# Long cross attention: rounds of two key tiles, with score halves issued beside peak halves and one visit to the full array in a round

## What is computed

```python
q = _rope((x_query @ Wq.T)...); k = _rope((x_kv @ Wk.T)...); v = (x_kv @ Wv.T)...
attn = softmax(einsum('bhqd,bhkd->bhqk', q, k) * SCALE)      # 56 queries x 1500 keys x 16 heads
out = einsum('bhqk,bhkd->bhqd', attn, v) ... @ Wo.T
```

## Time and profile before

| what | value |
|---|---|
| median of the three runs | 1459.55 us (1456.22 to 1461.99) |
| span of the profiled execution, first to last instruction | 1397.8 us |
| the profiled execution's own time end to end | not given; the median is 61.75 us above the span |
| TensorE matmuls busy, whole span | 1277.9 us, 91% |
| VectorE, ScalarE, GpSimd busy | 76%, 57%, 60% |
| first and last score load of the stage | 605.4 us, 1293.6 us |

### The profile page before, as it was taken

The page is one execution under the profiler, slowest core; times in us unless marked ns, Lnnn a source line. Parts: engine busy times, 40 slices in busy tenths (PEclk is TensorE's granted clock), DMA queues, the critical chain, the costliest instruction groups (busy, mean ns, idle before and its releaser), DMA issues.

```text
span 1397.8 us, 42378 instructions
## 1 busy us (share of the span) xinstructions
PE 1277.9 (91%) x17390; PEld 904.3 (65%) x17390; DVE 1066.3 (76%) x1817; ACT 802.5 (57%) x1760; POOL 842.5 (60%) x839
## 2 busy tenths in 40 slices
PE   6878999998997898678999999999999999988998
PEld 4556888788984666345565666656656666565986
DVE  6895676766677888777888888888888887886556
ACT  2542335336662333147677777777777777777541
POOL 6676232161567566578677786776777767665033
PEclk9887999999998999879999999999999999999999
DMA  5002700004521504546765465565565654546112
GB/s 139 2 1 68 244 3 2 2 28 131 163 59 29 78 12 89 104 133 134 156 136 145 118 129 134 113 139 130 112 145 133 114 139 96 120 85 186 43 49 54
DMA packets 84849, 136.19 MB, mean 97 GB/s; under 512 B 19809, under 2 KB 68322, under 8 KB 81314
## 3 DMA queue, kind: packets, MB, share of 16 engines
q1 hardware_dynamic: 80946, 125.87, 38.7%
q0 software_dynamic: 3712, 7.61, 1.9%
HBM read 98.38 MB, written 40.76 MB: 100 GB/s over the span
## 4 chain that ended last, share of the span: by engine, by line
PE 44%; ACT 6%; DVE 3%; issue 2%; POOL 2%; DMA 1%; ACTq 0%; POOLq 0%; SPq 0%; DVEq 0%
PE ps L2024 9%; PE ps L2040 8%; PE ps L1986 6%; PE ps L1977 6%; PE ps L2000 4%; ACT ARENA L2196 3%; ACT ARENA L2180 2%; PE ps L2502 2%; PE ps L2466 2%; DVE ARENA L2117 2%; PE ps L2513 1%; PE ps L2049 1%; PE ps L2476 1%; POOL ARENA L2245 1%; DMA key_parts<-ARENA 1%
## 5 line engine op out<-in xcount | busy, mean ns | idle before, releaser
L2117 DVE TENSOR_REDUCE ARENA<-ps 112x2 f32<-112x1000 f32 x384 | 456.3, 1197 | 109.7 <-PE ps L2000 108.0
L2196 ACT ACTIVATE ARENA<-ps 125x448 f32<-125x448 f32 x768 | 375.8, 546 | 106.5 <-PE ps L2024 103.7
L2245 POOL TENSOR_TENSOR ARENA<-ARENA 64x500 f32<-64x500 f32 x192 | 219.9, 1145 | 33.5 <-ACT ARENA L2174 9.1
L2024 PEld LDWEIGHTS ps<-ARENA 64*125 64x125 bf16 x3072 | 123.2, 134 | 143.3 <-ACT ARENA L2196 98.4
L2040 PE MATMUL ps<-ARENA 125*17 125x112 f32 x6144 | 210.3, 263 | 0.0
L2024 PE MATMUL ps<-ARENA 64*125 64x112 bf16 x3072 | 167.5, 228 | 28.7 <-ACT ARENA L2196 24.8
L2040 PEld LDWEIGHTS ps<-ARENA 125*17 125x17 f32 x6144 | 129.4, 97 | 57.3 <-issue 48.0
L2000 PE MATMUL ps<-ARENA 64*112 64x500 bf16 x768 | 153.7, 385 | 9.8 <-DVE ARENA L2117 8.9
L130 POOL TENSOR_TENSOR rs<-rs,mhalf 128x1 f32<-128x1 f32 x96 | 73.0, 762 | 122.4 <-DVE rs L125 122.1
L2251 POOL TENSOR_TENSOR ARENA<-ARENA 128x500 f32<-128x500 f32 x96 | 136.8, 1425 | 7.5
L2256 POOL TENSOR_TENSOR ARENA<-ARENA 128x500 bf16<-128x500 f32 x96 | 104.1, 1085 | 57.4 <-ACT ARENA L2180 57.4
(11 more groups left out here) (332 smaller groups left out, 2401.7 us busy)
## 6 DMA issues: line engine op xcount, KB each, us to landing
ARENA<-key_parts SPq DMA_DIRECT2D x192, 187.5 KB, 4.9
ARENA<-in_ctxT SPq DMA_DIRECT2D x96, 250.0 KB, 3.2
key_parts<-ARENA SPq DMA_DIRECT2D x64, 375.0 KB, 3.9
slots<-in_c_blank SPq DMA_DIRECT2D x2, 1472.0 KB, 12.8
results<-ARENA SPq DMA_DIRECT2D x42, 64.0 KB, 2.7
last_slots<-in_c_blank SPq DMA_DIRECT2D x1, 2144.0 KB, 12.5
ARENA<-in_L_ffn_W SPq DMA_DIRECT2D x1, 2048.0 KB, 8.5
ARENA<-in_L_ffn_W SPq DMA_DIRECT2D x4, 512.0 KB, 10.6
```

The source lines that it names most:

```text
L2024: m = e.matmul(ps[0:KT, b1[h], 112 * g:112 * g + 112], KS[b % 4][r, g, KT * kt:KT * kt + KT], Q1[r, b % 2, 112 * g:112 * g + 112], start=T ...
L2117: e.tensor_reduce(mxp[0:112, b % 2, 2 * g:2 * g + 2, ch], ps[0:112, b1:b1 + 2, 0:500], AX, ALU.max) \
L2196: e.activation(Pb[0:KT, n % NP_, 448 * h:448 * h + 448], ps[0:KT, b1[h], 0:448], ACT.Exp, bias=0.0, scale=1.0).then_inc(exped.sem, 1)
L2245: e.tensor_tensor(T2[r:r + 64, :], T0[64 - r:128 - r, n % 2, :], sin[64 - r:128 - r, sl], ALU.mult) \
```

## The change

The list `order()` now goes in rounds of two tiles m and m+1: score m, peak, score m+1, peak, then in one visit all steps of the kinds in VISIT (of both tiles: keys, values, full, fold, turn, out, finish and others), then apply m-2 and apply m-1. Steps of tile m that are not in VISIT stay between the two scores; those of tile m+1 come behind the visit. Banks are dealt out from the new list by the same rule.

On TensorE a score that is followed by a peak is now issued with it, by a new function. For each half h of the score: its first matmul, then one peak matmul of 500 columns in the other half of the rows, then the score's other three. The wait for a bank is made for each half by itself.

```diff
--- before.py
+++ after.py
@@ -1776,6 +1776,8 @@
                     f[10].append(("turn_slots", 1))
                 return f
 
+            VISIT = ("keys", "values", "full", "fold", "turn", "out", "finish", "query", "route", "count", "turn_slots")
+
             def order():
                 yield from (("clear", 0), ("mask", 0), ("mask", 1), ("keys", 2, 0), ("keys", 2, 1))
                 for k in range(12):
@@ -1793,26 +1795,26 @@
                     yield ("stack", 2, i)
                 for k in range(6):
                     yield ("peak", 1, k)
-                for n in range(B * NK + 2):
-                    b, kt = divmod(n, NK)
-                    if n < B * NK:
+                for m in range(0, B * NK + 2, 2):
+                    visit = []
+                    for n in (m, m + 1) if m < B * NK else ():
+                        b, kt = divmod(n, NK)
                         yield ("score", b, kt)
                         if kt < 6 and b + 1 < B:
                             yield ("peak", b + 1, 6 + kt)
                         if kt >= 6 and b + 2 < B:
                             yield ("peak", b + 2, kt - 6)
-                    steps = side(b)[kt] if n < B * NK else []
-                    short = [x for x in steps if kt % 2 and x[0] in ("full", "fold", "turn", "out", "finish", "query")]
-                    if n >= 3 and n % 2:
-                        yield ("apply", *divmod(n - 3, NK))
-                        yield from short
-                        yield ("apply", *divmod(n - 2, NK))
-                        if kt == 1:
-                            yield ("own", b - 1)
-                    singles = [x for x in steps if x[0] in ("keys", "values")]
-                    yield from singles
-                    yield from [x for x in steps if x not in short and x not in singles]
-                    if n == B * NK:
+                        steps = side(b)[kt]
+                        visit += [x for x in steps if x[0] in VISIT]
+                        if n % 2:
+                            yield from visit
+                        yield from [x for x in steps if x[0] not in VISIT]
+                    if m >= 2:
+                        yield ("apply", *divmod(m - 2, NK))
+                        yield ("apply", *divmod(m - 1, NK))
+                        if m % NK == 0:
+                            yield ("own", m // NK - 1)
+                    if m == B * NK:
                         yield ("begin", 0)
 
             def early(t):
@@ -2065,10 +2067,45 @@
                 elif kind in ("route", "count", "turn_slots", "begin"):
                     stages[5].parts["step_pe"](e, w, step, b1)
 
+            def score_beside_peak(e, w, step, beside):
+                b, kt = step[1:]
+                pb, p = beside[1:]
+                pg, ch = divmod(p, 3)
+                n, sb, pk = NK * b + kt, at[step], at[beside]
+                w.wait_ge(*ks_of(b))
+                w.wait_ge(*q_full(b + 1))
+                w.wait_ge(*ks_of(pb))
+                if pb == 3:
+                    w.wait_ge(*c2_in(2))
+                w.wait_ge(*masked(pb + 1))
+                for h in range(2):
+                    own, other = slice(64 * h, 64 * h + 64), slice(64 - 64 * h, 128 - 64 * h)
+                    if free[sb[h]]:
+                        w.wait_ge(*free[sb[h]])
+                    free[sb[h]] = exped(2 * n + h + 1)
+                    w.wait_ge(*free[pk + 1 - h])
+                    for g in range(4):
+                        m = e.matmul(ps[0:KT, sb[h], 112 * g:112 * g + 112], KS[b % 4][own, g, KT * kt:KT * kt + KT],
+                                     Q1[own, b % 2, 112 * g:112 * g + 112], start=True, stop=True)
+                        if g == 3:
+                            m.then_inc(scored.sem, 1)
+                        if g == 0:
+                            m = e.matmul(ps[0:112, pk + 1 - h, 0:500], Q0[other, pb % 3, pg].rearrange("p j s -> p (j s)"),
+                                         KS[pb % 4][other, pg, 500 * ch:500 * ch + 500], start=True, stop=True)
+                            if h:
+                                m.then_inc(peak_mm.sem, 1)
+                free[pk] = free[pk + 1] = peaked(12 * pb + p + 1)
+
             def pe(e, w):
                 w.wait_ge(*c1_in(len(loads)))
-                for step in order():
-                    pe_step(e, w, step)
+                steps = list(order())
+                taken = None
+                for step, after in zip(steps, steps[1:] + [("end", 0)]):
+                    if step[0] == "score" and after[0] == "peak":
+                        score_beside_peak(e, w, step, after)
+                        taken = after
+                    elif step != taken:
+                        pe_step(e, w, step)
 
             def early_pe(e, w, t):
                 for step in early(t):
```

## The result

The changed kernel takes 1475.65 us (median of four runs, 1470.9 to 1476.07) against 1457.88 us for the kernel before, timed beside it: a ratio of 1.0124, 95% interval 1.0094 to 1.0154. It is 18 us slower, where 22 us were forecast.

A forecast was written before the change was run, and what follows sets the result against it. TensorE's order of work was taken to set the pace. 24 batches at +0.98 (+23.6), +2 for batches 0 to 2 and 26, -2.7 and -1 at the end gave +22 on 1459.55: 1481.5 us, range 1464 to 1525.

The forecast's parts named there:

- The ring (Part 3): Three banks: second half of score m+1 and the visit wait for tile m's exponentials; visit starts at 1.62, not 1.02.
- Changes of shape (Part 2): TensorE's rounds have three changes of block shape for four: -0.13 us; fold, full, out, finish another -0.26; turn only -0.13.
- Halves (Part 1): Score halves issued beside peak halves on TensorE: each half still has 0.43 us to do, no gain booked.
- Other queues: GpSimd, VectorE, ScalarE's cast and SyncE: zero cost, covered by the longer round; otherwise a late cast holds the odd tile's exponentials.
- The sum: Whole kernel: 24 batches times 0.98 is +23.6, with the remaining batches and rounds together +22 us.
- The stage's remaining parts: Batches 0 to 2 and 26 take +2 together, nine rounds from batch 28 -2.7, the last nine rounds -1.
- Two readings of the old trace: TensorE's clock at nine tenths or more all through the stage; median of runs 61.75 us above the profiled span.
- The 61.75 us between the span and the median: Median of the runs over the profiled span of the kernel before; left alone, with the profile's end-to-end time not shown.
- A: On TensorE a long peak matmul holds back score matmuls behind it: +29 to +37 on top, say 1515; chance 0.17.
- B: Not slower: a lone half is through sooner, first exponential at 0.41 instead of 0.53, 1457.6 us; chance 0.10.
- C: The three banks do not bind as read: visit starts at 1.02, -110 us, 1372; chance 0.02.

The follow-up runs named there:

- Experiment 6: Changed kernel with exponentials of the long cross attention made on 224 of each half's 448 columns; 1440.71 us against 1470.91 for the changed kernel.
- experiment 8: Changed kernel with apply m-2 moved from the round's end to between the two scores; 1453.32 us against 1470.91 for the changed kernel, 1455.02 for before.
- experiment 4: Kernel before with score halves issued beside peak halves, but all bank waits ahead of the first matmul; 1455.26 us against 1453.18, ratio 1.0012.
- experiment 9: Changed kernel with an apply between the scores in rounds with a short step, keys or values there otherwise; 1439.05 us against 1455.02 for before, 0.9883.

## Why the prediction was right, point by point

**The ring (Part 3): right, and shown.** The visit was put at 1.62 after the opening, and starts at 1.58 (1.51 in the second round, 1.63 with keys alone); the second half was put at 1.19 and starts at 1.14. In the new trace TensorE goes on 0.05 after an exponential's end and not 0.11. In the second round the exponentials also start 0.06 earlier than in the others, as they did in the old trace (0.47 after the opening for 0.53). These two make up the 0.11 between the 3.47 of this round and the 3.58 worked out. Experiment 6 moves the visit by moving ScalarE alone, and experiment 8 makes 18 us good by covering the wait with work that was there. The old trace had shown the same wait without cover in batch 30, which is why no price had to be guessed.

**Changes of shape (Part 2): right in size.** The rounds come out as forecast: 3.97 with fold for 4.00, 3.56 with keys for 3.56, 3.70 with full for 3.72, 3.69 with turn for 3.75, 3.67 with finish for 3.68. From the visit's start on, 1.96 us pass in a round of values alone, which is the 1.07 and 0.89 worked out. No experiment changed the number of changes of shape alone.

**Halves (Part 1): right as far as it went, and incomplete.** I booked no gain for the interleaving, and experiment 4 shows that it has none in the old list. The separate wait was in the forecast where it matters for the change, as the first half of score m+1 ran ahead of the exponential. I missed that it also works on the old list, where it is worth 0.7 us a batch: I didn't cost that part of the change by itself.

**Other queues: one cover failed.** The prediction took zero and named the failure, a late cast that holds the odd tile's exponentials. It happened in the first round of odd batches: 4.00 for 3.87, as the visit's out waits again (0.17 at L2063). With 0.13 in every second batch it is small here and 1.0 us in experiment 9.

**The sum.** For a pair of batches +1.63 (0.93 and 0.70) against the +1.97 forecast, so 24 batches give +19.1 for +23.6, mostly the 0.05 to 0.1 on the visit. The stage's remaining parts were taken as -1.7 together, and the one pair of profiles on like chips has -1.1 there (-1.4, -2.3 and +2.6, where +2 for the first two and -3.7 for the last were forecast: both signs were wrong, and that the sum comes near is luck). That makes +18.0 for the stage where +22 was forecast, and the timed runs say 16 to 18.

**Two readings of the old trace.** The clock was not at nine tenths all through the stage: the slice from 594 to 629 us, in which it starts, has seven tenths. From 610 us on the share is full again but for short dips, and no term of the sum hung on it. The 61.75 us between the span and the median are not an end-to-end cost either. Where both numbers are of one execution they differ by under 2 us (1403.7 and 1401.9); the profile was of the faster kind of chip.

**The rivals.** A (a long matmul holds back short ones) falls with the trace above: the short ones start 0.10, 0.16 and 0.21 after the long one, and exponentials start 0.55 after the opening, not 0.64. Of the two rules of the Trainium skill that stood against each other, the trace agrees with the one on its page "TensorEngine Tiling (Array Packing)", section "Key Properties", that different tiles work in parallel, with the 0.55. It does not bear out a hold by the strict program order of the page "TensorE: Matmul & The Clock Gate", section "The mechanism", of the Trainium skill. Starts mostly keep that order here; in 166 of 732 cases the long matmul's recorded start lies 5 to 7 ns ahead of that of the short one which stands before it in the program. Whether ends keep the order the trace doesn't show, since the ends of matmuls are modelled. B would have needed an exponential that starts at 0.41; they start at 0.55, and at 0.48 in the second round. C would have shown no wait.

## What to carry to other kernels

When independent steps are regrouped to save changes of mode, write down for each buffer of a small ring who last read it and when: work that stood between two uses was the cover for that release, and here 0.13 us saved for each change of mode was paid for with a wait of about 0.5 us a round. Cost each part of a change alone, since one half of this one was worth 1.3% by itself and the other lost 3%. A wait split so that each half of a step asks only for its own buffer is cheap to try where two buffers come free one behind the other; here it gave 1.3%.

## What the runs showed of the hardware that was not expected

The same program took 1403 to 1406 us on one chip, and 1447 to 1458 us in all other sets of runs, on at least two other chips. The timeline of batches 4 to 25 was the same to a hundredth of a us for most of them; the difference lay in the stages before, in batches 29 and 30 (19.9 and 14.7 us on the one, 30.3 and 19.8 on the other) and behind the last score. Why is open; in the changed kernel's first profile the chain that ended last has 6.1 us in this stretch, at 1297 us, for which it names no engine of the core. A profile from one chip should not be compared by its span with one from another.
